# Attention and feed-forward layers on one core: another order of calls in five queues, and a quarter of the query blocks moved by DMA

## The reference

```python
def autocorrelation(q, v):            # 8 heads; transforms along the 128 rows
    corr = ifft(fft(q) * conj(fft(v))).real
    w, idx = top_k(corr, 9); w = softmax(w)
    return sum(w[i] * v[min(idx[i] + pos, 127)] for i in range(9))
x = x + autocorrelation(layernorm(x), ctx)              # a
x = x + experts(layernorm(x), W_base, 8 experts, rank 16, best 2)   # b
x = x + window_attention(layernorm(x), ctx)             # c: 8 heads of 16
x = x + experts(layernorm(x), 4 experts, rank 16, best 2)           # c
```

## Time and profile before

| what | value |
|---|---|
| time, median of 3 runs | 1870.63 us (1867.35 to 1871.33) |
| profiled execution | 1869.2 us, span 1867.4 us |
| PE busy | 1708.1 us (91%) |
| PEld, DVE busy | 1082.9 us (58%), 1569.8 us (84%) |
| ACT, POOL busy | 1165.5 us (62%), 905.9 us (49%) |
| DMA | 549359 packets, 111.37 MB; 531088 of them under 512 B |

### The profile page before, as it was taken

The page is one execution under the profiler, slowest core; times in us unless marked ns, Lnnn a source line. Parts: engine busy times, 40 slices in busy tenths (PEclk is TensorE's granted clock), DMA queues, the critical chain, the costliest instruction groups (busy, mean ns, idle before and its releaser), DMA issues.

```text
span 1867.4 us, 48204 instructions
## 1 busy us (share of the span) xinstructions
PE 1708.1 (91%) x19296; PEld 1082.9 (58%) x19296; DVE 1569.8 (84%) x4726; ACT 1165.5 (62%) x1929; POOL 905.9 (49%) x870
## 2 busy tenths in 40 slices
PE   3689999999999999999999999999999999999975
PEld 2356566666556666556666655666665566665553
DVE  6778898888889888888888888988888888888853
ACT  5257666666666665765666676666666566667642
POOL 2445544455554545555455555444555545455432
PEclk8799999999999999999999999999999999999985
DMA  5133322333332233332223333223334322333220
GB/s 208 34 58 69 58 50 48 54 69 69 69 48 47 54 61 69 69 58 53 48 51 69 69 69 57 49 48 55 69 69 64 51 48 48 67 69 58 29 30 24
DMA packets 549359, 111.37 MB, mean 60 GB/s; under 512 B 531088, under 2 KB 531344, under 8 KB 548624
## 3 DMA queue, kind: packets, MB, share of 16 engines
q1 hardware_dynamic: 549136, 108.29, 30.7%
HBM read 57.94 MB, written 16.78 MB: 40 GB/s over the span
## 4 chain that ended last, share of the span: by engine, by line
PE 56%; DVE 19%; ACT 9%; POOL 8%; issue 6%; DMA 1%; SPq 0%; DVEq 0%; ACTq 0%; POOLq 0%
PE pb L601 18%; PE pc L674 8%; ACT q_diag L876 6%; POOL rest L1422 4%; PE pa L561 4%; POOL prob L1422 4%; PE pa L523 3%; PE pa L497 3%; PE pa L524 3%; PE pa L498 3%; PE pa L499 3%; ACT v_im L778 3%; PE pb L590 2%; DVE rows_c L1249 2%; DVE x_c L1141 2%
## 5 line engine op out<-in xcount | busy, mean ns | idle before, releaser
L601 PE MATMUL pb<-w_base_h,even_words 128*128 128x512 f16 x1024 | 324.8, 379 | 0.0
L1459 POOL TENSOR_TENSOR sc<-sc,sc_rec 128x512 f32<-128x512 f32 x128 | 134.1, 1048 | 294.6 <-DVE sc_rec L1236 294.6
L876 ACT ACTIVATE q_diag<-sc,par 32x512 f32<-32x512 f32 x384 | 268.8, 715 | 10.3 <-DVE sc L1149 3.1
L1429 POOL TENSOR_TENSOR p_hl<-sc,p_hl 128x512 f16<-128x512 f32 x128 | 164.3, 1283 | 208.0 <-ACT p_hl L778 208.0
L601 PE MATMUL pb<-w_base_l,even_words 128*128 128x512 f16 x512 | 193.9, 379 | 0.0
L488 PE MATMUL pa<-xn_a,tab 128*128 128x512 f32 x384 | 181.7, 610 | 4.6 <-ACT xn_a L778 4.6
L674 PEld LDWEIGHTS pc<-sc_t,v_diag 128*128 128x128 f16 x6144 | 170.1, 97 | 20.6 <-DVE sc_t L1243 6.0
L674 PE MATMUL pc<-sc_t,v_diag 128*128 128x32 f16 x6144 | 173.9, 177 | 5.6 <-DVE sc_t L1243 5.6
L652 PE MATMUL pc<-k_h,q_diag 128*128 128x32 f16 x2048 | 169.2, 177 | 0.0
L653 PE MATMUL pc<-k_l,q_diag 128*128 128x32 f16 x2048 | 168.5, 177 | 0.0
L654 PE MATMUL pc<-k_h,q_diag 128*128 128x32 f16 x2048 | 168.5, 177 | 0.0
(11 more groups left out here) (166 smaller groups left out, 4619.6 us busy)
## 6 DMA issues: line engine op xcount, KB each, us to landing
x_a<-in_x SPq DMA_DIRECT2D x32, 512.0 KB, 5.5
x_res<-in_ctx_in SPq DMA_DIRECT2D x32, 512.0 KB, 5.1
x_res<-in_x SPq DMA_DIRECT2D x32, 512.0 KB, 3.7
v_diag<-even_words SPq DMA_DIRECT2D x128, 128.0 KB, 4.9
v_diag<-p_hl SPq DMA_DIRECT2D x128, 128.0 KB, 4.9
out<-rows_c SPq DMA_DIRECT2D x32, 512.0 KB, 2.6
v_diag<-in_base_w SPq DMA_DIRECT2D x4, 1024.0 KB, 10.0
q_diag<-in_ra SPq DMA_DIRECT2D x1, 544.0 KB, 13.7
```

The costliest lines, as they stand in the source:

```text
L601: mm(pb[:, h, :], rows[:, cols], weights[:, j, h * HALF:(h + 1) * HALF], start=(j == 0 and m == 0), stop=False)
L876: nc.scalar.activation(q_diag[rows, blocks, col:col + QB], source, ACT.Copy, scale=par[rows, a:a + 1]).then_inc(qd_out.sem, 1)
L1429: g_.tensor_tensor(part[:, :, :, LO], sc[:, g % 2, :, :], part[:, :, :, HI], ALU.subtract)\
```

## The change

Three things are changed. First, the order of the calls in the steps of all five engines. Second, GpSimd's quarter of the queries' blocks is gone; SP places it with two transfers from `q_hl` to `q_diag` (`place_queries`), and TensorE and VectorE wait for these (`q_placed`) where they waited for GpSimd (`qd_pool`). Third, waits that belong to the new order: `b_base` waits for the low halves of the features, `c_subtract` of groups 2 and 3 waits for GpSimd's low half of group g - 2, and the bare waits on GpSimd go. The core of the diff:

```diff
+            def place_queries(b):
+                sp.wait_ge(ql_out.sem, ql_out.after(b))
+                sp.wait_ge(qdiag_set.sem, 1)
+                if not first(b):
+                    sp.wait_ge(mm_sc.sem, mm_sc.after(b - 1))
+                for head in (2 * MOVED_PAIR, 2 * MOVED_PAIR + 1):
+                    rows = slice(HD * head, HD * (head + 1))
+                    sp.dma_start(q_diag[rows, :, rows], q_hl[rows, :].rearrange("p (n t) -> p n t", t=QB))\
+                        .then_inc(q_placed.sem, 16)
...
 # SP, step
                 if live(2):
                     place_values(i - 2, 0)
+                    place_queries(i - 2)
+                    place_values(i - 2, 1)
+                if live(3):
+                    store(i - 3)
+                if live(-1):
+                    load_ctx(i + 1)
                 if live(-1) and not first(i):
                     load_x(i + 1)
-                if live(2):
-                    place_values(i - 2, 1)
-                if live(-1):
-                    load_ctx(i + 1)
-                if live(3):
-                    store(i - 3)
...
 # TensorE, b_base and step
+                if part == 0:
+                    pe.wait_ge(xtl_out.sem, xtl_out.after(b))
...
+                if live(1):
+                    a_corr(i - 1, 0)
+                    a_corr(i - 1, 1)
+                    a_context_long(i - 1, 0, 1 - odd)
+                if live(2):
+                    b_base(i - 2, 1, 0)
+                if live(3):
+                    c_scores(i - 3, 2)
+                if live(1):
+                    a_context_long(i - 1, 1, 1 - odd)
                 if live(2):
                     b_router(i - 2)
                 if live(3):
+                    c_scores(i - 3, 3)
                     c_attend(i - 3, 0)
                 if live(2):
                     b_keys(i - 2, odd)
-                    b_base(i - 2, 1, 0)
-                if live(3):
-                    c_scores(i - 3, 3)
-                if live(2):
                     b_base(i - 2, 1, 1)
...
-                if live(0):
-                    a_corr(i, 0)
-                    a_context_long(i, 0, odd)
-                    a_corr(i, 1)
-                if live(2):
-                    c_scores(i - 2, 2)
-                if live(0):
-                    a_context_long(i, 1, odd)
...
 # ScalarE, step
+                if live(1):
+                    a_values(i - 1)
+                if live(3):
+                    b_query_blocks(i - 3, 0, 0, 1)
+                    b_query_blocks(i - 3, 0, 1, 1)
+                    b_query_blocks(i - 3, 1, 0, 1)
+                    b_query_blocks(i - 3, 2, 0, 1)
+                    c_exp(i - 3, 0)
+                    b_query_blocks(i - 3, 2, 1, 1)
+                if live(2):
+                    b_features(i - 2, 0)
...
 # VectorE, end of step
                 if live(0):
                     b_norm(i, 1, x1_out)
+                if live(2):
+                    c_result(i - 2, 1)
+                if live(0):
                     variance(i, 1)
...
                 if live(-1):
                     a_product(i + 1)
-                if live(2):
-                    c_result(i - 2, 1)
+                if live(-2):
+                    a_norm(i + 2)
                 if live(1):
                     c_sums(i - 1, 0)
                     c_scores(i - 1, 1)
+                if live(0):
+                    b_features(i, 0)
+                if live(1):
                     c_subtract(i - 1, 1)
                 if live(0):
-                    b_features(i, 0)
+                    b_features(i, 1)
+                if live(-2):
+                    variance(i + 2, 0)
                 if live(-1):
                     a_top(i + 1, 0)
-                if live(0):
-                    b_features(i, 1)
-                if live(1):
-                    c_transpose(i - 1, 0)
-                    c_sums(i - 1, 1)
-                    c_scores(i - 1, 2)
-                if live(-1):
-                    a_top(i + 1, 1)
```

More of the change, by code:

```diff
@@ L719, in step @@
                     b_values(i - 2, odd)
-                    b_base(i - 2, 0, 0)
                 if live(3):
@@ L723, in step @@
                 if live(2):
+                    b_base(i - 2, 0, 0)
                     b_base(i - 2, 0, 1)
@@ L961, in step @@
                 if live(3):
+                    c_high(i - 3, 1)
+                if live(2):
+                    experts_exp(i - 2, 0, pb, E0)
+                if live(3):
+                    c_high(i - 3, 2)
+                    c_attended(i - 3, 0)
+                if live(2):
+                    b_keys(i - 2)
+                if live(3):
+                    c_exp(i - 3, 3)
+                if live(2):
+                    experts_mid(i - 2, 0)
+                if live(3):
                     c_attended(i - 3, 1)
-                    c_high(i - 3, 3)
                 if live(0):
                     ctx_high(i, odd)
+                if live(3):
+                    c_high(i - 3, 3)
                 if live(2):
@@ L987, in step @@
                 if live(2):
-                    b_query_blocks(i - 2, 0, 0, 0)
                     b_query_blocks(i - 2, 2, 1, 0)
@@ L1279, in step @@
             def step(i, odd, live):
+                if live(0):
+                    a_top(i, 1)
+                    a_lead(i)
                 if live(2):
+                    c_sums(i - 2, 1)
+                    c_scores(i - 2, 2)
                     c_subtract(i - 2, 2)
+                    c_transpose(i - 2, 0)
+                    c_sums(i - 2, 2)
+                    c_scores(i - 2, 3)
                 if live(1):
@@ L1284, in step @@
                 if live(2):
-                    c_sums(i - 2, 2)
-                    c_scores(i - 2, 3)
-                if live(0):
-                    a_lead(i)
-                if live(2):
+                    c_subtract(i - 2, 3)
                     c_transpose(i - 2, 1)
-                    c_subtract(i - 2, 3)
                 if live(1):
@@ L1436, in a_normalise @@
                     .then_inc(prob_out.sem, 1)
-            pool_rows = slice(32 * POOL_PAIR, 32 * POOL_PAIR + 32)
-            def b_query_blocks(b, a, half):
-                if first(b) and a == 0 and half == 0:
-                    pool.wait_ge(qdiag_set.sem, 1)
-                if a == 0:
-                    pool.wait_ge(ql_out.sem, ql_out.after(b))
-                    if not first(b):
-                        pool.wait_ge(mm_sc.sem, mm_sc.after(b - 1, 2 * half + 2))
-                col = (2 * POOL_PAIR + a) * QB
-                blocks = slice(half * NBLK // 2, (half + 1) * NBLK // 2)
-                g_.tensor_tensor(q_diag[pool_rows, blocks, col:col + QB],
-                                 q_hl[pool_rows, :].rearrange("p (n t) -> p n t", t=QB)[:, blocks],
-                                 par[pool_rows, a:a + 1].unsqueeze(2).to_broadcast([32, NBLK // 2, QB]),
-                                 ALU.mult).then_inc(qd_pool.sem, 1)
-                pool.wait_ge(qd_pool.sem, qd_pool.after(b, 2 * half + a + 1))
             def c_normalise(b, g):
@@ L1472, in step @@
                 if live(1):
-                    b_query_blocks(i - 1, 1, 1)
+                    root(i - 1, 2)
+                if live(2):
+                    root(i - 2, 3)
                 if live(0):
+                    a_sum(i, 0)
+                    a_sum(i, 1)
                     root(i, 1)
-                if first(i - 0):
-                    clear_values()
-                if live(0):
                     b_bias(i)
-                if first(i - 0):
-                    clear_queries()
-                if live(0):
-                    pool.wait_ge(bias_added.sem, bias_added.after(i))
-                if live(0):
-                    pool.wait_ge(ln_rs[1].sem, ln_rs[1].after(i))
                 if live(1):
```

86 lines of the change are left out of this document (24 added, 62 removed).

## The result

The changed kernel takes **2042.03 us** (median; 2036.76 to 2047.56) against 1869.9 us for the kernel before on the same chip: a ratio of 1.092, 95% interval 1.089 to 1.095. The direction was forecast, the size was not: 2042 lies far above 1923 and outside 1880 to 1962. The profiled execution has a span of 2040.6 us, so it is 173 us above that of before.

What follows compares the result with a forecast made beforehand. TensorE's queue was taken as the bound. Late loads of x, 29 turns x 1.7 = 49.3 us, and ends of +3 on 1869.2 gave 1921.5; with 1.4 for the median, 1923 us, range 1880 to 1962.

Steps and rivals of the forecast that it cites:

- What bounds the kernel: TensorE's queue is the bound, busy 52.47 of 55.0 us in a period; only its 2.5 us of waits can be won.
- Part 1: VectorE's products before the correlation come earlier, shortening the period by 0.25 us (bounds 0 and 0.9).
- Part 2: Queries' quarter goes from GpSimd to SP: cost nothing, 1.5 us of cover; up to 1 us in a period if late.
- Part 3: load_x is last on SP but VectorE reads x earlier: x lands at 1062.2, TensorE waits 2.05 us per turn.
- The three large transfers: The store and the loads of context and x, behind the short pieces on SP; priced at 1.5 us each plus start-up.
- the argued start-up: Start-up of the load of x behind the store on SP, which may be partly hidden; taken as half hidden.
- Part 4: Rest of the turn up to the weights' transposes: no further TensorE wait, at worst 0.3 us; period grows by 1.7 us.
- Part 5: Start and end: later first products, a GpSimd memset moved; start between 0 and +9 us, +4 taken, last steps -1.
- A: Rival: x lands before 1060.1, so the period falls by 0.25 to 0.35 us; 1865, or 1860 us; chance 0.14.
- C: Rival: x late as forecast, and a Part 4 chain or the queries' landing adds 0.5 us or more; 1938 or more; chance 0.10.

Runs made afterwards that it cites:

- norm_back: The changed kernel with VectorE's a_norm and variance of x back at their old, later places and SP's order kept; 1867.2 us, ratio 0.998.
- before_quarter_sp: The kernel before with only the queries' quarter moved from GpSimd to two SP transfers, all orders as before; 1870.8 us, ratio 1.000.
- gpsimd_quarter: The changed kernel with the queries' quarter back on GpSimd and no queries' transfers on SP; 1904.8 us, ratio 1.017.
- fill_wait: The changed kernel with 14 added, unused matmuls per turn on TensorE ahead of b_base(1, 0), where it waits; 2003.5 us, ratio 1.071.
- norm_after_features: The changed kernel with VectorE reading x after the features, x still last on SP; 1909.3 us, ratio 1.021.
- x_before_queries: The changed kernel with load_x on SP moved ahead of the queries' two transfers; 1866.5 us, ratio 0.998.
- x_before_values: The changed kernel with load_x on SP moved between the queries' transfers and the second set of values; 1879.8 us, ratio 1.006.

## Why the prediction was wrong, step by step

**What bounds the kernel** and **Part 1** held. The new order makes the period 0.53 us shorter (54.97 to 54.44, norm_back), against 0.25 taken and a bound of 0.9. TensorE's wait before the correlation falls from 0.90 us to 0.35, and not to the 0.7 forecast.

**Part 2** held for its own question: the queries come in time, the scores wait for no DMA, and before_quarter_sp puts the price at nothing. GpSimd is busy 132.7 us less, 4.15 in each batch, near the 4.4 expected.

**Part 3** had the right mechanism, the right waiting instructions and the right release, and failed in its first term, the landing of `x`: forecast 2.2 us after the second product (1062.2 against 1060.0), measured 4.95. Of the 2.75 us, 2.5 stand ahead of the last of the values. By the forecast that lands at 1057.1, 2.9 before the product's end; it lands 0.4 before it. I had priced the two queries at 1.55 us by the rate of the values, and had the four values behind them as fast as if nothing were there: 7.7 us from their first issue to the last landing (1049.4 to 1057.1), for which I gave no working. Measured, SP is through with the two queries after 1.3 us, but their 128 KB take some 2.5 us of the DMA engines, and the four values take 10.2 us, against 7.9 in gpsimd_quarter and 8.8 before. SP's four issues take 6.6 us in the mean behind the queries and 4.8 without them. The three large transfers were put at 5.1 us and take 5.35. That part of the sum, with the argued start-up, was sound.

The point from which lateness costs was 0.1 us after the product by the forecast and is 0.46. That went the other way.

**The term that was missing** is the clock. I read "full granted clock" in the windows of before and priced TensorE's wait at its length. The wait itself slows what follows: twelve matmuls take 4.37 us and not 2.75, 1.6 us in a turn. fill_wait gives back 1.4 of them.

These add up. Against the forecast period (1.7 above before) the turn is longer by 2.75 (landing) + 1.6 (clock) - 0.36 (later point of decision) - 0.28 (larger gain of Part 1) = 3.7 us; measured are 161.5 - 49.3 = 112.2 us more than the sum had for the periods, 3.9 in each of 29 turns. The last 0.15 is in my own sum: a landing 2.1 us too late less 0.25 gained is 1.85 and not 1.7. At 2.2 us late the period would by the table have been 54.44 + 1.74 and a clock term between 0.1 and 0.8, 56.3 to 57.0; the forecast had 56.7. At that lateness the missing clock and the terms that were too high about cancel, which would have been luck; at 4.95 they do not. By my own sum the right landing would have given 1923 + 29 x 2.75 = 2003 us, and the clock would still have been missing.

**Part 4** held: the table's sum leaves under 0.1 us in a turn of the changed kernel for anything else. The slack of 0.3 us and less showed itself in norm_after_features.

**Part 5** named the right wait and counted too little. The first `x_c` comes 10.6 us later, against +4 and a bound of +9. I had 5 of 12 us won back by other waits, and 6.5 by the memset. The long instruction did not go, it became another one: beside the second memset VectorE has one of 8 columns, 0.17 us in the median of its 32 turns, which here ends with the memset:

```profile
88.00 6.41 DVE L1093 TENSOR_SCALAR neg_max<-top 128x8 f32<-128x8 f32 x1
87.46 6.93 POOL L1465 MEMSET q_diag<- 128x8192 f32 x1
```

The bad end of Part 5 had that (0 to 7). The early read of the second batch's `x`, 9.75 us of waiting once the constants are out of the way, was not in it at all.

**The rivals.** A is what happens when `x` is in time: it gave 1865 and 1860, and x_before_queries and norm_back took 1866.5 and 1867.2. C was the nearest to what came, "1938 or more", but by other means than it named. The range was too narrow because its two ends for the landing, 1061.4 and 1063.1, differed only in the start-up of the last load: the measure of four values and one load, 10.6 us, was taken in a queue without the new members, and their price had no bad end.

## What to carry to other kernels

A load that is moved back in a queue and a read that is moved forward are each free and together cost 9%: for each transfer write down the time at which it lands and the time at which its first reader comes, and give the landing a bad end, since what is new in the queue also slows the issue of what follows. Then look at what is queued behind the reader on its engine and who waits for that; moving the read behind five short calls was worth 133 us here. And a wait of some 4 to 5 us on TensorE should be priced with the slower matmuls behind it, 1.6 us here.

## What the runs showed that I had not expected

- An idle TensorE is dearer than its idle time: `b_base(1, 0)` began 4.5 us late in each turn, and its twelve matmuls then took 1.6 us longer. 14 useless matmuls in each turn of the wait made the kernel 38.6 us faster.
- Two transfers of 64 KB in pieces of 64 bytes between SBUF places moved some 50 GB/s with the DMA engines 0.56 busy, where others with the same pieces reach 80 to 88 at 0.80. The first of them delays what is behind it by 4.0 us (1.4 of them SP's wait for the queries), the second by only 1.0.
- SP's time to issue the same four DMAs is not a constant. In the mean it is 4.8 us in gpsimd_quarter, 5.6 behind `x` (before), 4.9 behind queries in long pieces, 6.6 behind them in short ones, and 8.1 behind those and `x` (x_before_values).
- A VectorE instruction of 8 columns, 0.17 us in the median, took 6.41 us beside GpSimd's memset of 8192 columns and ended with it. That the memset holds it is inferred from these two rows and from the 7.38 us in the earlier trace rows, not tested.
